# Last layer of a four-layer graph network: who adds up the eight relations of a node's own rows

## The reference

```python
out = x @ W_self + b_self
for r in range(8):                       # one attention head for each relation
    mask = concat([edge_type == r, ones(N)])      # each node also has a loop to itself
    h = x @ W[r];  s = h @ a_src[r];  d = h @ a_dst[r]
    e = leaky_relu(s[src] + d[dst], 0.2)          # -inf where masked
    alpha = softmax of e over the edges of one dst
    out = out + segment_sum(alpha * h[src], dst) + bias[r]
x = layernorm(x + out)
```

## Time and profile before

| | |
|---|---|
| median of three executions | 8430.0 us (8417.5 to 8430.58) |
| profiled execution | 8409.43 us, its span 8407.5 us |
| mean granted TensorE clock | 0.611 of 2.4 GHz |
| GpSimd busy | 5989.0 us (71%) |
| TensorE, VectorE, ScalarE busy | 3614.6, 3113.7, 1009.6 us |
| last layer's gathers | from 6128.2 to 8179.3 us |

### The profile page before, as it was taken

The page is one execution under the profiler, slowest core; times in us unless marked ns, Lnnn a source line. Parts: engine busy times, 40 slices in busy tenths (PEclk is TensorE's granted clock), DMA queues, the critical chain, the costliest instruction groups (busy, mean ns, idle before and its releaser), DMA issues.

```text
span 8407.5 us, 78987 instructions
## 1 busy us (share of the span) xinstructions
PE 3614.6 (43%) x14426; PEld 2885.7 (34%) x14427; DVE 3113.7 (37%) x5678; ACT 1009.6 (12%) x3308; POOL 5989.0 (71%) x6283
## 2 busy tenths in 40 slices
PE   3444333333344434444344343434512555555555
PEld 3333333332222222222222222222312454555555
DVE  3323232323223232323222222222444566666666
ACT  0000000000000000000000000000200233333335
POOL 7777777776777777776777777777267777777770
PEclk6566565555665656566565655656655666666667
DMA  2111111111222222222111111111444554554553
GB/s 58 31 30 30 30 30 30 30 30 42 54 56 57 55 58 55 58 55 48 28 29 28 29 28 29 28 29 28 136 112 102 125 141 128 138 132 129 139 139 86
DMA packets 575401, 546.64 MB, mean 65 GB/s; under 512 B 344667, under 2 KB 344667, under 8 KB 575008
## 3 DMA queue, kind: packets, MB, share of 16 engines
q0 software_dynamic: 200704, 212.34, 13.8%
q1 hardware_dynamic: 345920, 271.71, 11.7%
q10 hardware_dynamic: 28384, 58.61, 1.9%
HBM read 440.61 MB, written 100.74 MB: 64 GB/s over the span
## 4 chain that ended last, share of the span: by engine, by line
POOL 56%; issue 24%; DVE 8%; PE 4%; DVEq 3%; DMA 2%; ACT 1%; POOLq 1%; ACTq 0%; SPq 0%
POOL gat L776 56%; PE p_b L1388 2%; DVEq L331 1%; DMA trip<-in_type_w 1%; ACT msg L989 1%; DVE sel L2031 1%; DVE sel L2035 1%; PE p_a L1449 1%; PE p_a L1447 1%; DVE oh L1668 0%; PE p_all L1377 0%; DVE oht L2027 0%; DVE sum_t L2063 0%; DVE dtab L2128 0%; ACT spare L1036 0%
## 5 line engine op out<-in xcount | busy, mean ns | idle before, releaser
L776 POOL DMA_INDIRECT gat<-x_d,idx x3136 | 2966.3, 946 | 1018.0 <-issue 1018.0
L776 POOL DMA_INDIRECT gat<-rel_d,idx x1568 | 1535.3, 979 | 685.7 <-issue 632.6
L776 POOL DMA_INDIRECT gat<-in_x,idx x1568 | 1485.5, 947 | 486.7 <-issue 486.7
L1668 DVE SCALAR_TENSOR_TENSOR oh<-dstf,fine_col,p_b 128x512 f32<-128x512 f32 x1578 | 1107.3, 743 | 381.9 <-issue 342.5
L1251 PE MATMUL p_all<-oh,gat 128*128 128x256 f32 x1568 | 720.6, 640 | 1194.6 <-DMA gat<-x_d,idx 1153.6
L1251 PE MATMUL p_all<-oh,msg 128*128 128x256 f32 x1568 | 714.5, 635 | 1183.4 <-DVE oh L1668 1183.4
L1237 PE MATMUL p_all<-oh,msg 128*66 128x128 f32 x3136 | 703.1, 417 | 1188.4 <-DVE oh L1668 1188.4
L1237 PEld LDWEIGHTS p_all<-oh,msg 128*66 128x66 f32 x3136 | 637.8, 230 | 1251.7 <-issue 1096.0
L1251 PEld LDWEIGHTS p_all<-oh,gat 128*128 128x128 f32 x1568 | 488.9, 327 | 1423.9 <-issue 1115.5
L1251 PEld LDWEIGHTS p_all<-oh,msg 128*128 128x128 f32 x1568 | 486.1, 325 | 1399.8 <-issue 1080.4
L1388 PE MATMUL p_b<-oh,msg 128*72 128x128 f32 x3136 | 664.7, 400 | 81.5 <-ACT msg L989 35.8
(11 more groups left out here) (275 smaller groups left out, 3344.1 us busy)
## 6 DMA issues: line engine op xcount, KB each, us to landing
he_d<-gat ACTq DMA_DIRECT2D x196, 288.0 KB
ea<-he_d SPq DMA_DIRECT2D x196, 288.0 KB
ea<-in_edge_attr SPq DMA_DIRECT2D x196, 256.0 KB, 2.7
gat<-x_d,idx POOLq DMA_INDIRECT x3136
drow<-dst_d SPq DMA_DIRECT2D x196, 256.0 KB
spare<-rel_d SPq DMA_DIRECT2D x98, 288.0 KB
gat<-in_x,idx POOLq DMA_INDIRECT x1568
gat<-rel_d,idx POOLq DMA_INDIRECT x1568
```

Source lines behind the costliest of these rows:

```text
L776: nc.gpsimd.indirect_dma_start(out=gat[:, q, s, :] if width == HROW else got[:, q, s, :], out_offset=None, in_=table, in_offset=bass.Indir ...
L1668: return vec.scalar_tensor_tensor(out=oh[:, u, cut, :], in0=bc(dst.unsqueeze(2), P, S // 2, W), scalar=fine_col[0:P, bass.ds(at, 1)], in1= ...
```

## The change

The reduce over relations leaves VectorE. For each tile of self rows TensorE issues eight products of the 128x128 identity (stationary) with `own5[k][:, r, :]` (moving, 128x64), which add up in the tile's columns of `y5`. VectorE then reads `y5` in place of `all5`. For the last block VectorE still scales.

Since `y5` is now in use up to block step 13, the turning of the next block's x rows, which goes through the same bank, is moved: SyncE's load from block step -8 to 0, TensorE's transposes and ScalarE's copies from block step -6 to 1. TensorE there waits for the sum of squares of the block before (`s_sqrt_in`), and the first tile's products wait until VectorE has read `y5` (`s_xfree`). ScalarE's scaling of a tile waits, as before, on `s_tile5`, which TensorE now raises.

```diff
--- before.py
+++ after.py
@@ -619,11 +619,11 @@
 
             def last_layer(it, i, lo):
 
-                b = last_block(it, i, lo, 6 - CH)
+                b = last_block(it, i, lo, 0)
                 if b is not None:
                     if lo > READY:
                         wait_for(sp, s_xfree[5], b + 2)
-                    c = (i - READY + CH - 6) // CH
+                    c = (i - READY) // CH
                     sp.dma_start(x5, rows(x3_d, b)).then_inc(s_xs[c % 2], 16)
                 for tt in range(BT):
                     b = last_block(it, i, lo, 4 + tt)
@@ -1008,7 +1008,7 @@
 
             def last_layer(it, i, lo):
 
-                b = last_block(it, i, lo, 8 - CH)
+                b = last_block(it, i, lo, 1)
                 if b is not None:
                     pairs = BT // 2 * W
                     wait_for(act, s_tr[5], b + 1)
@@ -1429,12 +1429,12 @@
 
             def last_layer(it, i, lo):
 
-                b = last_block(it, i, lo, 8 - CH)
+                b = last_block(it, i, lo, 1)
                 if b is not None:
-                    c = (i - READY + CH - 8) // CH
+                    c = (i - READY - 1) // CH
                     wait_for(pe, s_xs[c % 2], it * 16 + 16 * (c // 2 + 1 + NI * turn_loads[5]))
-                    if lo > READY:
-                        wait_for(pe, s_xfree[5], b + 2)
+                    if lo > READY + 1:
+                        wait_for(pe, s_sqrt_in, b + roots_upto[5])
                     for t in range(0, BT, 2):
                         pair = x5[:, t:min(t + 2, BT), :].rearrange("p t d -> p (t d)")
                         width = pair.shape[1]
@@ -1449,6 +1449,16 @@
                         ins = nc.tensor.matmul(y5[:, t, 0:D], xt[0:D, 0, nth5(t):nth5(t) + W],
                                                wself2[0:D, :], start=False, stop=(t == BT - 1))
                     ins.then_inc(s_mid[5], 1)
+                for tt in range(BT):
+                    b = last_block(it, i, lo, 6 + tt)
+                    if b is not None:
+                        k = (i - READY - 6 - tt) // CH * BT + tt & 1
+                        if tt == 0:
+                            wait_for(pe, s_xfree[5], b + 3)
+                        wait_for(pe, s_own5, b * BT + (tt + 1))
+                        for r in range(R):
+                            ins = nc.tensor.matmul(y5[:, tt, 0:D], ident[:, :], own5[k][:, r, :], start=(r == 0), stop=(r == R - 1))
+                        ins.then_inc(s_tile5, 1)
 
             def look_and_sum(it, i, lo):
                 t = it * BODY + i
@@ -2157,22 +2167,18 @@
                     dve.sem_inc(s_xfree[5], 1)
                 for tt in range(BT):
                     b = last_block(it, i, lo, 6 + tt)
-                    if b is not None:
+                    if b is not None and lo >= READY + (NB - 1) * CH:
                         c = (i - READY - 6 - tt) // CH
                         k = c * BT + tt & 1
-                        if lo < READY + (NB - 1) * CH:
-                            wait_for(dve, s_own5, b * BT + (tt + 1))
-                        else:
-                            wait_for(dve, s_h5[k], tile_load(it, c, tt))
-                            vec.tensor_tensor(own5[k], h5[k][:, :, 0:D], bc(self_w[:, tt, :].unsqueeze(2), 128, R, D), ALU.mult)\
-                                .then_inc(s_own5, 1)
-                            wait_for(dve, s_own5, b * BT + (tt + 1))
-                        vec.tensor_reduce(out=all5[:, tt, :], in_=own5[k].rearrange("p r d -> p d r"), op=ALU.add, axis=AX.X)\
-                            .then_inc(s_tile5, 1)
+                        wait_for(dve, s_xfree[5], b + 3)
+                        wait_for(dve, s_h5[k], tile_load(it, c, tt))
+                        wait_for(dve, s_tile5, b * BT + (tt - 1))
+                        vec.tensor_tensor(own5[k], h5[k][:, :, 0:D], bc(self_w[:, tt, :].unsqueeze(2), 128, R, D), ALU.mult)\
+                            .then_inc(s_own5, 1)
                 b = last_block(it, i, lo, 13)
                 if b is not None:
                     wait_for(dve, s_tile5, b * BT + BT)
-                    ch(vec.tensor_tensor(base5, base5, all5, ALU.add))
+                    ch(vec.tensor_tensor(base5, base5, y5[:, :, 0:D], ALU.add))
                     ch(vec.tensor_reduce(out=r1[:, :], in_=base5, op=ALU.add, axis=AX.X))
                     ch(vec.scalar_tensor_tensor(out=base5, in0=rows5(r1), scalar=-1.0 / D, in1=base5,
                                                 op0=ALU.mult, op1=ALU.add))
```

## The result

The median went from 8427.2 us (8413.1 to 8434.52) to 8441.02 us (8428.75 to 8450.32), twenty executions each: +13.8 us, ratio 1.0018 [1.0011, 1.0024]. I had forecast +16. A second timing on another chip gave 1.0022 [1.0013, 1.0031]. The profiled execution has a span of 8426.9 us, 19.4 more than before.

What follows compares the result with a forecast made beforehand. The prediction took GpSimd's gathers and the issue pause between them as the bound. Its terms, -10 while gathers run, +9 after them and +17 at the end, gave +16 us: median 8430 to 8446, whole range 8412 to 8478.

Steps and rivals of the forecast that it cites:

- The end, +17: After the last sum: two leftover tiles +2.2, the turn +1.9, the last block's seven tiles +13; bounds +6.6 and +24 us.
- the rival's 4.9: Price in us of a tile's sixteen product instructions at the low clock if weight load and product don't overlap; chance 0.17.
- Rival 1: Last block's products run at the high clock, 1.9 us a tile; end +6.6, sum about 0, 8430 us; chance 0.15.
- After the gathers, +9: From the gathers' end to the last sum: three terms, together +9 us, bounds 0 and +22.
- (a): After the gathers: the 5.14 us waits behind the turn go at steps 196, 210 and 224, together -10.6 us.
- (b): After the gathers: the moved turn is paid at steps 203 (+2.3 us) and 217 (+4 us).
- (c): Steps 196 to 227: products of 18 tiles cost +13.5 us in sum, VectorE's saving already off.
- While gathers run, -10: Last layer's gathers: 10 of GpSimd's 39.5 us of waits for indices won; bounds +3 and -22 us.
- Rival 4: While gathers run, TensorE's products delay the look-up and VectorE sets the pace: +3 us a block, 8486 us; chance 0.08.
- Rival 2: The turn held GpSimd back; nearly all its stops go, -36 of 39.5 us; sum -19.5, 8410 us; chance 0.15.
- Rival 3: Weight load and product don't overlap: last block +23, the tail's products +10 more, 8467 us; chance 0.17.

Runs made afterwards that it cites:

- the move alone: The changed kernel without TensorE's products (VectorE reduces every tile, the turning stays moved), against the kernel before: 0.9963, 0.996 and 0.9979 on three chips.

## Why the prediction was right, and where its steps were off

The range, the sign and the size held (+16 forecast, +13.8 measured), but two of the three terms were off and cancelled: the gathers by +7.6 us, what follows them by -7.6. That the sum came within 3 us is luck.

Split by halves instead, the forecast reads: the move -10 - 4.3 + 1.9 = -12.4 us, the products 0 + 13.5 + 15.2 = +28.7. By the stretches the move gave -7.8 - 5.0 + 2.3 = -10.5 us and the products 5.4 + 6.4 + 14.9 = +26.7. Both halves were right in size; what was wrong is where the products' cost falls.

**The end, +17: right, term by term.** The whole is +17.2. The move alone has 44.2 us there, +2.3, which is the turn between the root and the copies (forecast 1.9). The rest, 14.9, is the products': from the end of the last sum to the addition of the block's halves 3.6 us instead of 1.5, so 2.1 for two tiles (forecast 2.2), and 12.8 for the last seven (forecast 13). The price of 3.5 us a tile was 24.12 / 7 = 3.4, and the rival's 4.9 was for products whose row counts alternate; these don't. One reading was wrong without harm to the sum: the last block's 11.5 us before were not paced by its loads. VectorE's seven reduces of 1.01 us and six scalings of 0.69 fill 11.2 of them.

**The clock.** The last block ran at 0.50 throughout, as the 28 products ahead of it had the earlier trace rows. Rival 1, by which sustained work lifts the clock, falls here: TensorE was busy for 24.00 of 24.00 us. With four products of 512 columns ahead, the same tiles ran at 1.00. The same kind of tile had run at 1.00 just before, beside the last sums:

```profile
8364.00:8373.00 9.00, 8.74 (x79) 8.60 (x79) 0.57 (x2) 5.67 (x25) 0.00 (x0) 1.00 0.12 29
```

Then TensorE stood 3.59 us, until block 12's sum of squares let it turn the last rows, and it came back at 0.50. The Trainium skill, TensorE: Matmul & The Clock Gate, "What's actually happening", says that the clock is throttled by default and that activity releases it. The last block does not agree, 24.00 us busy at 0.50; the kernel with the four added products does.

**After the gathers, +9: the mechanism right, a size off.** Measured +1.4. The move alone gives the split, since it has terms (a) and (b) and no products: 181.4 instead of 186.4, -5.0, where (a) and (b) were -10.6 + 6.3 = -4.3. TensorE's sums of the kernel after show both signs; steps 196, 210 and 224 with the sums behind them, then 217 and 218:

```profile
8199.97 1.94 PE L1388 MATMUL p_b<-oh,msg 128*72 128x128 f32 x16 [1.58 <-DVE sum_t L2073]
8204.93 1.94 PE L1388 MATMUL p_b<-oh,msg 128*72 128x128 f32 x16 [1.29 <-DVE sum_t L2073]
...
8286.86 1.92 PE L1388 MATMUL p_b<-oh,msg 128*72 128x128 f32 x16
8288.61 1.90 PE L1460 MATMUL p_a<-spare,ident 128*128 128x64 f32 x16
8291.25 1.97 PE L1388 MATMUL p_b<-oh,msg 128*72 128x128 f32 x16 [0.73 <-ACT msg L989]
...
8322.01 3.63 PE L1388 MATMUL p_b<-oh,msg 128*72 128x128 f32 x16 [3.29 <-ACT msg L989]
8325.45 0.63 PE L1441 MATMUL p_a<-ident,w_rbias 128*128 128x128 f32 x4
8329.31 3.42 PE L1388 MATMUL p_b<-oh,msg 128*72 128x128 f32 x16 [3.23 <-ACT msg L989]
...
8355.92 1.97 PE L1388 MATMUL p_b<-oh,msg 128*72 128x128 f32 x16 [0.73 <-ACT msg L989]
8357.72 1.90 PE L1460 MATMUL p_a<-spare,ident 128*128 128x64 f32 x16
8359.89 1.97 PE L1388 MATMUL p_b<-oh,msg 128*72 128x128 f32 x16 [0.27 <-ACT msg L989]
```

The stops of 5.14 us are gone, and the sum after step 217 waits 3.23 us for ScalarE's weighing, which stands behind the copies: the step takes 7.30 us instead of 3.28. Step 224 takes 3.97 instead of 7.55, as forecast. The mis-sized step is (c): +13.5 for the products was +6.4 (187.8 less 181.4). I had taken the low clock in part of them; but the products filled TensorE's pauses, and most rows of L1460 in this stretch are 1.90 us, the high clock. What (c) costs hangs on the pauses beside it: once the copies stand a step later and the pauses behind the turn are gone, the products cost 14.1 us by the table. That the pauses are the reason is argued, not tried.

**While gathers run, -10: the term that was off.** Measured -2.4. The move was worth 7.8 (GpSimd's waits for indices 39.5 to 24.7 us) and the products, which I had put at nothing here, took 5.4 of it back (24.7 to 37.5). I had written that ScalarE's scaling "now waits for TensorE's tile before last instead of VectorE's, which has about the same place in the step". It has not: the products stand last in TensorE's step, and L1036 waited 100.4 us for them where it had waited 11.5 us for VectorE. I had looked for the products' harm at the look-up, for which VectorE waits, and not at the release of `own5`. Both are there: against the move alone ScalarE waits 21.5 us more at L1036 and VectorE 31.6 us more for the look-up, and with doubled products both waits grow again. At the look-up the term was mis-sized too, since I had held VectorE's saved 7.2 us a block to outweigh it. Rival 4 had the harm by the look-up alone, and much larger than it was. Which of the two ways makes GpSimd's indices late is not shown.

**The other rivals.** Rival 2, the turn as what held GpSimd back, named a true cause: without products the gathers gain 7.8 us, and with the copies a step later 14.4 (of its 36). But its time of 8410 needed the products to be free. Rival 3 falls by the 3.4 us a tile.

What stays open: the stretches are from single profiles on different chips. They repeat within some 4 us in the one pair of the changed kernel, but on the chips that take 10,465 us by more: the two kernels that differ from each other only in the last block have 2902.5 and 2913.0 us of gathers, and 196.9 and 206.9 after them, on the same chip. So the split of the gathers into 7.8 and 5.4 is known only roughly. The sign of each half of the whole change is surer, since it rests on timings: the move alone is a gain on three chips, and the products a loss against it on two. Nor is it tried whether the products would cost less if they stood earlier in TensorE's step.

## What to carry to other kernels

When work moves to another engine, find who waits for its buffers and for what stands behind it, and read where in the new engine's own order it stands: besides its cost of 1.9 to 3.4 us against 1.03 it made ScalarE's buffer and VectorE's look-up late. A change with two halves is priced and timed as two; here the half that was only there to make room was a gain of 0.2 to 0.4%, and the half that was meant was the loss. And work at the very end of a kernel has no cover: the 17 us lost there are more than the whole change lost (13.8), so the last block may deserve another form than the others.

## What the runs showed of the hardware

**The clock did not rise for 112 instructions of 64 columns back to back.** 24.00 us fully busy at a granted 0.50; after eight instructions of 512 columns (5.4 us, mean grant 0.63) the next 96 of the same kind as the 112 ran at 1.00. A tile cost 3.4 us at the one level and 1.8 to 1.9 at the other.

**The same kernel before takes 10,465 us on some chips.** There the first three layers are longer too: the last layer's gathers begin at 7321.1 us in the run of the move alone, against 6128.2. The gather itself is not slower:

```profile
L776 POOL DMA_INDIRECT gat<-rel_d,idx x1568: 938/944/2535, 7321.1 to 10200.5; - x196
```

The page of that run, the chain that ended last, and the waits from 8000 to 10200 us:

```profile
another core or an unknown queue 33%; issue 33%; DVE 14%; DVEq 12%; PE 5%; POOL 2%; ACT 1%; DMA 1%; SPq 0%; ACTq 0%; POOLq 0%
```

```profile
POOL gat L776 <- DMA idx<-key_d: 733.5, 73, 18.1
...
DVE sum_t L2063 <- remote: 475.5, 40, 21.4
...
ACT msg L987 <- remote: 280.0, 31, 21.0
```

GpSimd stands 733.5 us for indices, and VectorE and ScalarE stand for a releaser that the trace can't name ("remote"; a program on one core has no other). Here GpSimd is no longer the pace. What the releaser is, no run shows. The order of the kernels was the same on these chips, the move alone fastest and the products at a cost. Its size can't be carried from one kind of chip to the other: the move alone took off 35.0 and 47.2 us there and 14.9 here, though the ratios, 0.9963, 0.996 and 0.9979, have intervals that overlap.
